# Sandwich kernel with a gated recurrence and routed experts: y's squares summed on ScalarE, its norm behind the next scan, block norms ahead of the weight lows

## The reference

```python
x = x + layernorm(attn(layernorm(x), W_in, W_gate, b_gate, rms_w, W_out))
x = x + layernorm(ffn(layernorm(x), router, gate_up, down, biases))

# attn: x is 16 sequences of 256 tokens of width 256; 4 heads of 64
gates = (x @ W_in.T) @ W_gate.T + b_gate        # i, f, o, c per head
i, f, o, c_t = exp(i), sigmoid(f), sigmoid(o), tanh(c_t)
c = f * c + i * c_t                              # along the sequence
h = o * tanh(c * rsqrt(mean(c * c) + 1e-6) * rms_w)
y = h @ W_out.T
# ffn: 16 experts, each token goes to its top 4
logits = x @ router.T + b; weights = softmax(top 4)
out = sum over the 4 of weight * (down(glu(gate_up(x))) + bias)
```

## Time and profile before

| | us |
|---|---|
| median of 3 runs (lowest, highest) | 800.43 (793.66, 808.10) |
| the profiled execution | 786.95 |
| its span, first to last instruction | 785.1 |
| busy: PE, DVE, ACT, POOL | 657.3, 540.5, 461.0, 395.9 |
| first scatter-add of the expert stage | 372.75 |
| mean granted TensorE clock | 0.877 of full speed |

### The profile page before, as it was taken

How to read it: one execution, slowest core, us unless ns; L and a number is a source line. 1 busy time by engine, 2 the same in 40 slices (tenths; PEclk the granted TensorE clock), 3 DMA queues, 4 the chain that set the end, 5 groups by cost and what they waited for, 6 DMA issues and landing times.

```text
span 785.1 us, 13641 instructions
## 1 busy us (share of the span) xinstructions
PE 657.3 (84%) x3818; PEld 424.8 (54%) x3818; DVE 540.5 (69%) x1595; ACT 461.0 (59%) x933; POOL 395.9 (50%) x300
## 2 busy tenths in 40 slices
PE   5988989599999846389799999999999999977450
PEld 2445646375665535246466666666666666644330
DVE  3626687768798877676477777777777776640992
ACT  2777786447567524235566777766777766650242
POOL 0012214754746626666666666666665656564111
PEclk9989998879999956579899999999999999995555
DMA  7966854699523212546677777777776766655987
GB/s 246 422 248 103 173 89 72 213 317 347 176 88 115 87 65 75 165 144 235 103 109 116 109 109 114 109 108 111 116 116 96 115 109 101 104 61 84 350 150 104
DMA packets 111897, 115.29 MB, mean 147 GB/s; under 512 B 31731, under 2 KB 101507, under 8 KB 110163
## 3 DMA queue, kind: packets, MB, share of 16 engines
q0 software_dynamic: 35456, 50.35, 38.0%
q1 hardware_dynamic: 76370, 64.07, 27.1%
HBM read 55.07 MB, written 59.31 MB: 146 GB/s over the span
## 4 chain that ended last, share of the span: by engine, by line
PE 45%; DMA 16%; DVE 15%; POOL 7%; issue 6%; ACT 6%; SPq 2%; POOLq 0%; ACTq 0%; DVEq 0%
DMA sums<-arena 10%; POOL routed L954 6%; PE PS L668 6%; PE PS L667 6%; PE PS L666 6%; PE PS L525 5%; PE PS L558 3%; PE PS L674 3%; PE PS L655 3%; PE PS L687 3%; PE PS L686 3%; PE PS L688 3%; PE PS L550 2%; ACT arena L740 2%; DMA W<-w_dn 2%
## 5 line engine op out<-in xcount | busy, mean ns | idle before, releaser
L980 POOL DMA_INDIRECT sums<-arena x144 | 222.8, 1547 | 127.2 <-DMA sums<-arena 61.1
L954 POOL DMA_INDIRECT routed<-arena,small x128 | 142.8, 1116 | 95.4 <-DVE small L1202 50.9
L1373 DVE TENSOR_SCALAR arena<-PS,small 128x256 f32<-128x256 f32 x144 | 78.4, 544 | 101.5 <-ACT arena L913 101.1
L525 PE MATMUL PS<-arena 128*128 128x512 f32 x256 | 127.5, 640 | 6.0 <-ACT arena L740 5.4
L740 ACT ACTIVATE arena<-PS 128x512 f16<-128x512 f16 (+1 forms) x180 | 105.3, 591 | 35.5 <-PE PS L566 15.0
L913 ACT ACTIVATE arena<-PS,small 128x256 f32<-128x256 f32 x144 | 68.2, 474 | 90.8 <-PE PS L668 90.4
L666 PE MATMUL PS<-W,arena 128*128 x288 | 111.2, 386 | 0.2 <-DVE arena L1375 0.2
L667 PE MATMUL PS<-W,arena 128*128 x288 | 111.1, 386 | 0.0
L668 PE MATMUL PS<-W,arena 128*128 x288 | 110.9, 385 | 0.0
L740 ACT ACTIVATE arena<-PS,arena 128x256 f32<-128x256 f32 x144 | 69.5, 483 | 33.6 <-DMA sums<-arena 29.4
L686 PE MATMUL PS<-W,arena 128*128 x288 | 79.1, 275 | 7.1 <-DVE arena L1363 5.7
(11 more groups left out here) (180 smaller groups left out, 1073.4 us busy)
## 6 DMA issues: line engine op xcount, KB each, us to landing
arena<-routed SPq DMA_DIRECT2D x144, 128.0 KB
W<-w_gu SPq DMA_DIRECT2D x8, 1024.0 KB, 23.4
W<-neg_mem POOLq DMA_DIRECT2D x16, 512.0 KB, 8.6
sums<-zero SPq DMA_DIRECT2D x2, 4096.0 KB, 26.1
W<-sums SPq DMA_DIRECT2D x16, 512.0 KB, 8.8
X<-x SPq DMA_DIRECT2D x8, 512.0 KB, 4.7
W<-w_dn SPq DMA_DIRECT2D x4, 1024.0 KB, 11.3
out<-X SPq DMA_DIRECT2D x8, 512.0 KB, 2.9
```

Of the source, the lines that this page charges most:

```text
L525: last = mm(PS[:, 2 + c % 2, :], WcT[:, k, c * P:(c + 1) * P], xT[:, k, :], start=(k == 0), stop=(k == KT - 1))
L954: pool.indirect_dma_start(routed, bass.IndirectOffsetOnAxis(ap=idx, axis=0), rows[b][:, jk // TOPK, :], None).then_inc(rows_sent[lane], 16)
L980: pool.indirect_dma_start(sums[j % SUMS], bass.IndirectOffsetOnAxis(ap=dst[j % MU], axis=0), yb[u], None, compute_op=ALU.add).then_inc(y_s ...
L1373: L.send(v.tensor_scalar(up[j % 2], acc[:, FF:2 * FF], gu_hi, gu_lo, ALU.min, ALU.max))
```

## The change

- W_out's transpose is made mean-free over its 256 columns once, in the prologue, so y has mean zero.
- ACT does not normalise y any more. In the same place (c = 7) it squares the four tiles of y with the sum in an accumulator (`square_y`, `ysq`), and waits for y alone.
- `y_stats` is now one operation of 4 columns on `ysq`. It and `y_norm` move from the end of step s − 1 to step s, behind the scan and ahead of the residual.
- `residual` reads y from PSUM and does scaling and addition in one operation per tile. PE's `rms_spread` waits for it instead of for `norm_y`, because it writes the same banks.
- `block_norms` moves ahead of the first `low` and of the statistics of x. The norms of x of blocks 5 to 7 are so made one step later, and `norm_x` moves from c = 1 to c = 5 for these blocks.

```diff
...
             def out_product(t):
                 pe.wait_ge(h_ready, t + 1)
+                if t == 0:
+                    pe.wait_ge(wr_ready, 4)
                 for j in range(BT):
                     for q in range(PAIRS):
                         last = mm(PS[:, 4 + j // 2, (j % 2) * DIM:(j % 2 + 1) * DIM], hT[:, q, j * P:(j + 1) * P],
...
                 act.wait_ge(cn_ready, t + 1)
                 nc.scalar.activation(cn, cn, ACT.Tanh, scale=rmsw).then_inc(tanh_ready, 1)
-            def norm_y(t):
-                act.wait_ge(r2_ready, t + 1)
+            def square_y(t):
+                act.wait_ge(y_mm, t + 1)
                 if t:
                     act.wait_ge(log_mm, t)
                 for j in range(BT):
                     last = nc.scalar.activation(yn[:, j, :], PS[:, 4 + j // 2, (j % 2) * DIM:(j % 2 + 1) * DIM],
-                                                ACT.Identity, bias=mr2[:, j:j + 1], scale=r2[:, j:j + 1])
-                last.then_inc(yn_ready, 1)
+                                                ACT.Square, accum_out=ysq[:, j:j + 1])
+                last.then_inc(ysq_ready, 1)
             def evac_x2(t):
                 for k in range(KT):
...
                     if new:
                         gate_chunk(s, c)
                     if c == CHUNKS - 1 and mid:
-                        norm_y(s - 1)
+                        square_y(s - 1)
                     if c == CHUNKS - 1 and old:
                         row_high(s - 2)
-                    if c == 1 and on(s, -1):
+                    if c == (1 if s + 1 < XRING else 5) and on(s, -1):
                         act.wait_ge(r1_ready, (1, 2, 3, 3, 3, 4, 5, 6)[s + 1])
                         norm_x(s + 1)
                     if c == 3 and mid:
...
             v.tensor_copy(ident16[:, :], ident).then_inc(ident16_ready, 1)
             v.tensor_copy(KB[:, :], KBf).then_inc(kb_ready, 1)
             L(v.tensor_copy(dest, K[:, C_DEST:C_DEST + BT]))
+            L(v.tensor_reduce(wo_mean, WoT, AX, ALU.add))
+            L(v.tensor_scalar(wo_mean, wo_mean, 1.0 / DIM, None, ALU.mult))
+            for q in range(PAIRS):
+                v.tensor_scalar(WoT[:, q, :], WoT[:, q, :], wo_mean[:, q:q + 1], None, ALU.subtract).then_inc(wr_ready, 1)
             dve.wait_ge(s_x[1], 16)
             stats_x(1)
             norms_x(BT, 2 * BT)
...
                 L(v.tensor_scalar(nv[:, 0:BT], mv[:, :, 1], eps, None, ALU.add))
             def residual(t):
-                dve.wait_ge(yn_ready, t + 1)
-                L(v.tensor_tensor(block_x(t), block_x(t), yn, ALU.add))
+                for j in range(BT):
+                    last = v.scalar_tensor_tensor(block_x(t)[:, j, :], PS[:, 4 + j // 2, (j % 2) * DIM:(j % 2 + 1) * DIM],
+                                                  r2[:, j:j + 1], block_x(t)[:, j, :], ALU.mult, ALU.add)
+                last.then_inc(res_done, 1)
+                dve.wait_ge(res_done, t + 1)
                 stats(lambda j: block_x(t)[:, j, :], mv3, LN_EPS)
             def block_norms(t, mid, old, ahead):
...
             def y_stats(t):
-                dve.wait_ge(y_mm, t + 1)
-                stats(lambda j: PS[:, 4 + j // 2, (j % 2) * DIM:(j % 2 + 1) * DIM], mv2, 4 * LN_EPS)
-
-            def y_norm(done=r2_ready):
+                dve.wait_ge(ysq_ready, t + 1)
+                L(v.tensor_scalar(nv[:, 0:BT], ysq, 1.0 / DIM, 4 * LN_EPS, ALU.mult, ALU.add))
+
+            def y_norm():
                 a, b, y, x = na[:, 0:BT], nb_[:, 0:BT], ny[:, 0:BT], nv[:, 0:BT]
                 n = L.send(v.tensor_scalar(a.bitcast(i32), x.bitcast(i32), 1, None, ALU.logical_shift_right))
...
                     n = L.send(v.scalar_tensor_tensor(r2 if turn == 2 else y, b, 1.5, y, ALU.add, ALU.mult))
                 yield
                 L.wait(n)
-                v.scalar_tensor_tensor(mr2, mv2[:, :, 0], -1.0, r2, ALU.mult, ALU.mult).then_inc(done, 1)
             def scale_cell(t):
                 dve.wait_ge(rb_mm, t + 1)
...
                 if s == 4:
                     scales(0)
                 if old:
+                    y_stats(s - 2)
+                    list(y_norm())
                     residual(s - 2)
                 if on(s, 3):
                     row_low(s - 3)
+                if mid or old:
+                    block_norms(s - 1, mid, old, s + 1 if XRING <= s + 1 < NBLK else 0)
+                if s == 1:
+                    scales(1)
                 if s in (2, 3, 4, 5, 6, 7, 8):
                     low()
-                ahead = s + 2 if XRING <= s + 2 < NBLK else 0
-                if ahead:
-                    dve.wait_ge(s_x[ahead], 16)
-                    stats_x(ahead)
-                if mid or old:
-                    block_norms(s - 1, mid, old, ahead)
-                if s == 1:
-                    scales(1)
+                if XRING <= s + 2 < NBLK:
+                    dve.wait_ge(s_x[s + 2], 16)
+                    stats_x(s + 2)
                 if on(s, 3):
                     list(row_tails(s - 3))
                 if s in (2, 3, 5, 6, 7, 8):
...
                     choose(s - 2)
                 if s in (1, 2, 3, 4, 5, 6, 7, 8):
                     low()
-                if mid:
-                    y_stats(s - 1)
-                    list(y_norm())
                 if s == 3:
                     peak_row(0)
                 if s == 8:
...
```

More of the change, by code:

```diff
@@ L243, in build @@
         st2 = tiny(BT * 6).rearrange("p (j s) -> p j s", s=6)
-        mv2 = tiny(BT * 2).rearrange("p (j s) -> p j s", s=2)
         mv3 = tiny(BT * 2).rearrange("p (j s) -> p j s", s=2)
@@ L247, in build @@
         rs = tiny(BT + BT * HEADS + BT)
-        r2, mr2, mr3 = tiny(BT), tiny(BT), tiny(BT)
+        r2, ysq, mr3 = tiny(BT), tiny(BT), tiny(BT)
+        wo_mean = tiny(PAIRS)
         rT = tiny(P, parts=BT * HEADS)
@@ L301, in build @@
         cn_ready, tanh_ready, h_ready = sem("cn_ready"), sem("tanh_ready"), sem("h_ready")
-        y_mm, r2_ready, yn_ready = sem("y_mm"), sem("r2_ready"), sem("yn_ready")
+        y_mm, ysq_ready, res_done = sem("y_mm"), sem("ysq_ready"), sem("res_done")
         r1_ready, r3_ready = sem("r1_ready"), sem("r3_ready")
@@ L543, in rms_spread @@
                 if t:
-                    pe.wait_ge(yn_ready, t)
+                    pe.wait_ge(res_done, t)
                 keep_busy(6, 4)
```

## The result

The changed kernel took 815.9 us (median of 4 runs, 814.37 to 817.71), the kernel before 797.04 us beside it (4 runs, 788.65 to 808.10). The ratio is 1.026, with an interval of 1.022 to 1.031: slower, by 18.9 us. Forecast were 822 and +22. A second set of runs gave 807.21 against 789.24 us, a ratio of 1.030 (1.021 to 1.039), +18.0. A ratio and its interval compare fast executions alone while the medians are over all, so the two need not agree: in the second set the kernel before has 5 fast executions of 10, with a median of 785.85, and against these the change costs 21 us.

The account below looks back on a forecast made before the run. The prediction took the path to `slots(5)` of step 8, on which POOL's scatters hang, as the bound. Its terms gave +19 there, plus 3 for PE's clock: +22 on 800.4, 822 us, range 798 to 836.

Parts of the forecast that it names:

- What decides: POOL's scatters run unbroken from block 5 to the expert stage, so only the delay of step 8's `slots(5)` counts: +19.
- The stall of step 4 swallows all: DVE's 3.06 us wait for x[6] in step 4 absorbs the lateness of steps 1 to 3, leaving +0.2.
- y's norm on the path, 2.4 a step: On DVE, y's norm no longer runs beside PE's gates but behind gate 7, on the path: +2.4 in every step.
- Accumulators +0.9 a step: On ScalarE, reading an accumulator costs 0.2 to 0.3 us per square, four per step: +0.9 (bounds 0.4 and 1.2).
- Detour: ScalarE's `high` waits for DVE's low, now behind the norms, delaying `rms_row`: +2.7, less 1.2, in steps 2, 3, 5, 6, 7.
- `norm_x`: Moved to c = 5, it makes PE's transposes of x at c = 7 wait: +2.0 in each of steps 4 to 6.
- Clock +1 a step: Longer PE waits in steps 5 to 7 lower its clock: +1 each (bounds 0 and 3.4), +3 in all.
- rival 2: PE's clock falls in steps 5 to 7 as in step 3: 19 + 3 × 3.4, +29, 829; chance 0.12.
- W_out's centring 0: About 1.3 us of DVE in the prologue, covered by its wait for gate 5 at the first scan: 0.
- Step 8, −4.1 and back: The late scan's 4.1 us before step 8's residual goes; +2.4 and +0.4 return, −1.2 and +1.3 about cancel: +19 at `slots(5)`.
- Rival 1: The wait over `high` and `norm_x` both hide, leaving 3.7 per step in steps 5 to 7: +11, 811; chance 0.22.
- rival 3: DVE's load from scan to `slots` sets the pace and is lightened: 786, or 800 in a weaker form; chance 0.16.

Follow-up runs that it names:

- e2: The changed kernel with the first weight low of each step back ahead of the block norms; 797.00 us against 787.00 for the kernel before, ratio 1.012.
- e6: Only y's chain changed; low, x statistics and `norm_x` as in the kernel before; 805.65 us against that kernel's 789.24, ratio 1.025.
- e3: The changed kernel with x's statistics ahead of the norms and `norm_x` at c = 1 again; 810.08 us against 787.00 for the kernel before, ratio 1.030.
- e9: The changed kernel with only y's squares moved ahead of gate 5; 788.66 us against 783.97 for the kernel before, ratio 1.012.
- e4: The changed kernel with y's squares ahead of gate 5, y's statistics and norm ahead of the scan; 784.54 us against 787.00 for the kernel before, ratio 0.997.
- e5: The changed kernel run and profiled again, without an edit; 807.21 us against 789.24 for the kernel before, ratio 1.030.
- e8: The changed kernel with unread filler matmuls in PE's waits for the norms and `rms_row`; 805.29 us against 789.24 for the kernel before, ratio 1.028.

## Why the prediction was right, and where its terms were off

- **What decides** was right: `slots` of block 5 in step 8 is 21.7 us late, and the first scatter-add came at 392.10. That the expert stage adds nothing is shown by the rest of the execution: 414.2 us before (416.7 and 414.8 in the other two profiles), 414.9 and 416.4 after. In the other runs it lies between 411.9 (e2) and 416.0, but for the 421.0 of e6.
- **The stall of step 4 swallows all**: the sum was right (+0.2 forecast; `rms_row` of step 4 at 156.24 against 156.25, 159.89 and 156.66), the sentence wasn't. The stall moves with the lateness and swallows none of it, as e3 shows; the low, the statistics and the wait left the norms' way, and happened to be worth as much as the lateness.
- **y's norm on the path, 2.4 a step**: it took 2.4 to 2.65 us between DVE's wake-up and the residual. e9 against e4 prices its place at 10.6 us in all, but only 3.7 of them in steps 5 to 8. The dearer part is one that the forecast had as given: the squares stayed behind gate 7, where `norm_y` had been, and DVE now waits 5.5 us for them in steps 5 to 7 instead of about 1; with the squares ahead of gate 5 the first scatter-add comes 15.5 us earlier (e9). **Residual +0.4**: 1.66 us against 1.23.
- **Accumulators +0.9 a step** was wrong. Each read takes about 0.25 us, but it starts while its activation's end is still on record, and the squares, which have no scale and bias from memory, are themselves shorter (0.40 us each; `norm_y`'s about 0.6; that it is the operands and not the function is not shown): four squares with their reads take 1.6 us (260.26 to 261.84) where `norm_y` took 1.95. The term is −0.35. From the squares of width 1024 I had taken the price of a read, and added it to `norm_y`'s time as if squares without scalars were otherwise no shorter.
- **Detour** (+1.5 net a step; 1.7 measured in e2) and **`norm_x`** (+2.0 in steps 4 to 6) were about right. In e5 against e3 the stretch from `rms_row` to the residual is 2.5 us longer in each of steps 4, 5 and 6, in e2 against e6 2.4, 2.3 and 0.6.
- **Clock +1 a step** was too small. From `rms_row` to `out_product` steps 5 to 7 took 9.8, 10.8 and 9.9 us instead of 7.6, 7.3 and 7.5, 8.1 longer where the forecast had 1.8 (3 for the clock, less 1.2 of slack). With e8's fillers they took 8.3, 6.7 and 6.9, so this is the clock's part. The accumulators had 1.25 us too much at each of four ends, 5 in all. That the two errors cancel, and the total comes out at 21.7 for 22, is luck. The wake-ups of steps 6 and 7 lie 39.9 us apart, outside the 33 to 37 that the forecast named as a sign.

  The trace shows 0.56 to 0.66 granted in steps 5 to 7, which is mostly 1.2 GHz, where the kernel before had 0.89 to 1.00, with some 3 us at 1.2 GHz in each of steps 5 and 7, under `out_product`. In step 6 that is 1.7 us at `rms_spread` and 0.9 at the transposes of x2, and the stretch grew by 5.2 us where 3.4 were forecast. In step 5 it grew by 2.3 only: the kernel before had a slow piece there itself, an `out_product` of 5.39 us instead of 3.70. The Trainium skill (TensorE: Matmul & The Clock Gate, Part 1) says that half the pulses pass behind idle time and all after sustained work; here PE stood 3.1 and 2.65 us ahead of `rms_spread` in step 6 and got the low level, stood 1.0 us in the kernel before and kept the high one, and with e8's fillers got it back. By that rule rival 2 held in steps 5 to 7. Its level of the clock did; its total (+29) did not, since it priced the clock at 3.4 a step (its own rows, 10.2 and 7.3, give 2.9), where 7.4 us in all came back with the fillers, and kept the accumulators. Waits are not all of it: in steps 5 and 7 of the kernel before PE stood 1.5 and 1.1 us, and fell to the low level all the same, 8 to 9 us later.
- **W_out's centring 0**: `rms_row` of step 1 is at 54.58 (e5), and at 53.57, 54.59 and 54.54 in the three profiles of the kernel before; some 1 us can't be told from nothing.
- **Step 8, −4.1 and back**: the late scan did take up the lateness of the squares: they were done at 296.3, 22.5 late, and the residual started at 299.24, 21.3 late. It is the one place where the new order wins.
- **The absolute time**, 822 against 815.9: 3 us are the size of the effect (18.9 against 22), 3 the base (800.43 is the median of three executions, 797.04 that of the same three and a fourth).

Rival 1 (the detour hides) is out by e2, rival 3 by DVE's waits for the squares, 5.5 us in each of steps 5 to 7 (4.5 and 3.4 in steps 2 and 3). The forecast's sign was such a wait at every step; in steps 4 and 8 there is none. Not settled are the standstill of the first profile, and why the first set of runs is 8 to 9 us longer for both kernels than the second.

## What to carry to other kernels

Work that is taken from an engine's load isn't taken from the path: without y's statistics DVE only waited longer for ScalarE (5.5 us instead of 1 in steps 5 to 7), and the norm behind that wait is 2.4 to 2.65 us of the path. Ask of each part on which side of the wait it lands: with squares and norm ahead of it, the same idea is 26 us faster.

Longer waits of PE cost again by its clock (1.9 us a step here, on average), and fillers win it back only where they are not themselves in the way. A stall for a DMA forgives lateness only if the DMA's own start doesn't depend on what is late; here it did (issued 4.2 us later in the changed kernel). What helps is to put the work that needs the load behind the path's.

## What was not expected of the hardware

- An ACTIVATE with Square of width 256 from PSUM with a sum read out takes 0.36 us from start to start (0.42 and the read's 0.25, overlapping), four of them 1.6 us; four with Identity and scale and bias from memory take 1.95.
- PE at 1.2 or 2.4 GHz: 16 matmuls with 16 rows in and 128 columns took 3.77 and 2.05 us, 8 transposes 1.97 and 1.09. 16 matmuls of 256 columns took 3.70 us at 2.4 GHz, 5.39 with some 3 us of it at 1.2 GHz, and 5.97 in step 8, where the low clock lasted longer.
- In one execution two engines stood until 160.0 for 6.74 and 13.27 us, though PE's work for them was over by 151.3 on record; it is in none of the 13 other profiles.
